# Message layer of a graph network: a PSUM bank per slot, and GpSimd's gathers and scatters in blocks of four

## The chip, the cores and the metric

The kernel runs on 1 core of one Trainium2 chip. The metric is the time of one execution on the device in microseconds; lower is better.

## The reference, cut to what matters

Four graph layers are applied to a table of 50,000 nodes with 128 features each, over 25,000 edges sorted by destination; each adds its result to the table and normalizes the rows. The change is in the last one, the message layer:

```python
x = _layernorm(x + _L3_gnn_ref(x, edge_weight, src, dst, L3_gnn_Wm, ...), axis=-1)

def _L3_gnn_ref(z, edge_weight, edge_src, edge_dst, Wm, bm, W1, b1, W2, b2):
    Wd, Ws, ww = (Wm[:H], Wm[H:2 * H], Wm[2 * H])
    msgs = z[edge_dst] @ Wd + z[edge_src] @ Ws + edge_weight[:, None] * ww[None, :] + bm
    agg = jax.ops.segment_max(msgs, edge_dst, num_segments=n)
    agg = jnp.where(deg[:, None] > 0, agg, jnp.zeros((), dtype=z.dtype))
    hidden = jax.nn.relu(z @ W1a + agg @ W1b + b1)
    return hidden @ W2 + b2
```

## The kernel before, in words

The program runs its stages one after the other: a prelude (weights folded, tables of edges), the dense pass over all nodes together with the first edge layer, then the edge layers PNA, attention and message. Nodes without an edge are finished in the dense pass; an edge layer computes the rows that have edges. `message_edges` is the last stage.

It walks the edges backward in 49 groups of 512 (`GROUP`), each four tiles of 128 edges. For a group: four gathers on GpSimd fetch the source rows (`gsrc.tile`, one indirect DMA of 128 rows of 512 bytes each, line 1603); SyncE loads the group's own rows, the edge weights and a row of flags. TensorE turns the source rows (TURN_SRC) and own rows (TURN_OWN) with four transposes each, ScalarE copies them to SBUF (COPY_SRC, COPY_OWN), TensorE forms the messages (SOURCE, two products of 512 columns in fp32, listed as two instructions each), VectorE takes the running maximum with one scan (SCAN), which starts from the last column of the group before. TensorE multiplies own rows (OWN, with the constant rows) and the maximum (HIDDEN) into one bank, ScalarE applies the ReLU, TensorE makes the output rows (PRODUCT, eight instructions of 128 columns, line 335), VectorE adds the own rows (RESIDUAL), and the layer norm follows: SQUARE (ScalarE), SUM (VectorE), ROOT (ScalarE), NEWTON (four small operations, VectorE), SCALE (four activations, ScalarE). Last, GpSimd writes the rows with four indirect DMAs (SCATTER0 to SCATTER3, line 2491).

All tiles have two copies, called slots; group n uses slot n mod 2. Of the PSUM banks, those for the hidden and the output rows have two copies, the one that takes the turned source rows and then the messages (`bank_src`) and the one for turned own rows (`bank_own`) have one each.

The order on every engine comes from a software pipeline, `pipelined`. `AT` gives each step a planned time after its group's start, `PERIOD` the distance between two groups. A step's place in a round is its time modulo the period, its age in rounds the quotient; every engine issues its own steps in that order, and waits on semaphores settle the rest. The planned times have no effect but this order. So before the change, in round n (the number is the group's age):

```
GpSimd   FETCH0(0) SCATTER0(4) FETCH1(0) SCATTER1(4) FETCH2(0) SCATTER2(4) FETCH3(0) SCATTER3(4)
TensorE  TURN_SRC(1) TURN_OWN(1) PRODUCT(2) SOURCE(1) OWN(1) HIDDEN(1)
ScalarE  SCALE(3) COPY_SRC(1) COPY_OWN(1) SQUARE(2) ROOT(2) RELU(1)
VectorE  RESIDUAL(2) SCAN(1) SUM(2) NEWTON(2)
SyncE    LOAD_OWN(0) LOAD_ROWS(0)
```

FETCH0 waits until the slot's earlier source rows are turned, SCATTER0 until its group is scaled (`norm.normed`), SCALE until the slot's earlier scatters have landed. The steady rounds run in a loop on each engine; the first and the last rounds are written out.

Of the kernel before, what the change touches and what calls it, by code (L numbers as in the profile page):

```python
# [87 lines left out]
def wait(eng, sem, count):  # L88

    if not (isinstance(count, int) and count == 0):  # L90
        eng.wait_ge(sem, count)  # L91
# [73 lines left out]
def backward(ap):  # L165

    return ap[:, ::-1]
# [150 lines left out]
def transpose_tiles(pe, out, rows, ident):  # L318

    for t in range(TPG):  # L320
        mm = pe.transpose(out[:, t:GROUP:TPG], rows[:, t * P:(t + 1) * P], ident[:])  # L321
    return mm
# [2106 lines left out]
def message_edges(nc, A, D, W, Ed, plan):  # L2429


    S, rounds = plan.ES, plan.E_ROUNDS
    mem = Mem(nc)
    rows = lambda n: [mem.sb(f"m_{n}{s}", [P, GROUP]) for s in range(S)]
    src, own, srcT, ownT, mx, h, y, x4 = (rows(n) for n in ("src", "own", "srcT", "ownT", "mx", "h", "y", "x4"))
    wrow = [mem.sb(f"m_wrow{s}", [1, GROUP]) for s in range(S)]
    low = [mem.sb(f"m_low{s}", [P, GROUP], BF16) for s in range(S)]
    bank_src, bank_own = mem.ps("m_bsrc"), mem.ps("m_bown")
    bank_hid, bank_out = ([mem.ps(f"m_b{n}{s}") for s in range(S)] for n in ("hid", "out"))
    norm = Norm(mem, "mn", S, 1, by_scalar=True)  # L2440
    gsrc = Gather(mem, "mg", S, Ed.src_first, D["x3"], src)
    (src_turned, src_copied, made, scanned, own_turned, own_copied, own_made, hidden, relued, out_made, residual, own_loaded,
# [8 lines left out]

    (FETCH0, FETCH1, FETCH2, FETCH3, LOAD_OWN, LOAD_ROWS, TURN_SRC, COPY_SRC, SOURCE, SCAN, TURN_OWN, COPY_OWN, OWN, HIDDEN,
     RELU, PRODUCT, RESIDUAL, SQUARE, SUM, ROOT, NEWTON, SCALE, SCATTER0, SCATTER1, SCATTER2, SCATTER3) = range(26)
    AT = (0, 2.5, 5.1, 7.6, 5.6, 6.1, 11.7, 14.2, 14.9, 17.1, 12.2, 14.7, 16.8, 18.6, 19.8, 22.9, 25, 25.9, 28.5, 29.4, 29.8,
          33.3, 41.9, 44.4, 47, 49.5)
    PERIOD = 10.2
    FETCH = (FETCH0, FETCH1, FETCH2, FETCH3)
    SCATTER = (SCATTER0, SCATTER1, SCATTER2, SCATTER3)

    with nc.Block() as block:  # L2460
        @block.sync
        def _(sp):
            def step(k, s, i):
                g = group(i, s)
                if k == LOAD_OWN:
                    wait(sp, own_turned[s], i)
                    wait(sp, residual[s], i)
                    mem.settle(sp)
                    sp.dma_start(own[s][:], tin[g + plan.DG]).then_inc(own_loaded[s], 16)
                if k == LOAD_ROWS:  # L2470
                    wait(sp, made[s], i)
                    wait(sp, scanned[s], i)
                    mem.settle(sp)
                    sp.dma_start(wrow[s][:], A["w_row"][bass.ds(g, 1), :]).then_inc(row_loaded[s], 16)
                    sp.dma_start(low[s][:], low_row[:, bass.ds(g * GROUP + 1, GROUP)].to_broadcast([P, GROUP])).then_inc(row_loaded[s], 16)

            pipelined(sp, plan.EG, S, PERIOD, AT, step)

        @block.gpsimd
        def _(pool):  # L2480
            def step(k, s, i):
                if k == FETCH0:
                    wait(pool, src_turned[s], i)
                if k in FETCH:
                    gsrc.tile(pool, s, FETCH.index(k), group(i, s))
                if k == SCATTER0:
                    wait(pool, norm.normed[s], i + 1)
                if k in SCATTER:
                    t = SCATTER.index(k)
                    at = group(i, s) * TPG + t  # L2490
                    pool.indirect_dma_start(  # L2491
                        out=D["out"], out_offset=bass.IndirectOffsetOnAxis(ap=Ed.out_first[:, at:at + 1], axis=0),
                        in_=x4[s][:, t * P:(t + 1) * P], in_offset=None, bounds_check=plan.N - 1, oob_is_err=False,
                    ).then_inc(stored[s], 16)

            pipelined(pool, plan.EG, S, PERIOD, AT, step, tail=rounds)
            for s in range(S):
                pool.wait_ge(stored[s], in_slot(plan.EG, S, s) * 16 * TPG)

        @block.tensor  # L2500
        def _(pe):
            def step(k, s, i):
                if k == TURN_SRC:
                    gsrc.arrived(pe, i, s)
                    wait(pe, scanned[s - 1], before(i, s))
                    transpose_tiles(pe, bank_src, src[s], W.ident).then_inc(src_turned[s], 1)
                if k == SOURCE:
                    wait(pe, src_copied[s], i + 1)
                    wait(pe, row_loaded[s], 32 * i + 32)
                    pe.matmul(bank_src[:], W.msg_src[:], srcT[s][:], start=True, stop=False)  # L2510
                    pe.matmul(bank_src[:], W.msg_w[:], wrow[s][:], start=False, stop=True).then_inc(made[s], 1)  # L2511
                if k == TURN_OWN:
                    wait(pe, own_loaded[s], 16 * i + 16)
                    wait(pe, own_copied[s - 1], before(i, s))
                    transpose_tiles(pe, bank_own, own[s], W.ident).then_inc(own_turned[s], 1)
                if k == OWN:
                    wait(pe, own_copied[s], i + 1)
                    wait(pe, relued[s], i)
                    wait(pe, residual[s], i)
                    pe.matmul(bank_hid[s][:], W.w1a_edge[:], ownT[s][:], start=True, stop=False)  # L2520
                    const_rows(pe, bank_out[s], W, C_MSG).then_inc(own_made[s], 1)
                if k == HIDDEN:
                    wait(pe, scanned[s], i + 1)
                    pe.matmul(bank_hid[s][:], W.w1b[:], mx[s][:], start=False, stop=True).then_inc(hidden[s], 1)  # L2524
                if k == PRODUCT:
                    wait(pe, relued[s], i + 1)
                    rows_matmul(pe, bank_out[s], h[s], W.w2_msg[:], stop=True).then_inc(out_made[s], 1)

            pipelined(pe, plan.EG, S, PERIOD, AT, step)

        @block.scalar
        def _(act):
            def step(k, s, i):
                if k == COPY_SRC:
                    wait(act, src_turned[s], i + 1)
                    wait(act, made[s], i)
                    act.copy(srcT[s][:], bank_src[:]).then_inc(src_copied[s], 1)
                if k == COPY_OWN:
                    wait(act, own_turned[s], i + 1)
                    wait(act, own_made[s], i)  # L2540
                    act.copy(ownT[s][:], bank_own[:]).then_inc(own_copied[s], 1)
                if k == RELU:
                    wait(act, hidden[s], i + 1)
                    wait(act, out_made[s], i)
                    act.activation(h[s][:], bank_hid[s][:], ACT.Relu, bias=W.b1_msg[:, 0:1]).then_inc(relued[s], 1)  # L2545
                if k == SQUARE:
                    wait(act, residual[s], i + 1)
                    norm.square(act, i, s, 0, tiles(y[s][:]))
                if k == ROOT:
                    norm.root_by_scalar(act, i, s, 0)  # L2550
                if k == SCALE:
                    wait(act, norm.inverted[s], 4 * i + 4)
                    wait(act, stored[s], i * 16 * TPG)
                    norm.scale_by_scalar(act, i, s, 0, x4[s], y[s])

            pipelined(act, plan.EG, S, PERIOD, AT, step)

        @block.vector
        def _(dve):
            norm.set_eps(dve, began)  # L2560
            dve.memset(mx[S - 1][:], 0.0).then_inc(began, 1)
            dve.wait_ge(began, S + 1)

            def step(k, s, i):
                if k == SCAN:
                    wait(dve, made[s], i + 1)
                    wait(dve, scanned[s - 1], before(i, s))
                    wait(dve, row_loaded[s], 32 * i + 32)
                    wait(dve, hidden[s], i)
                    dve.tensor_tensor_scan(backward(mx[s]), backward(low[s]), backward(bank_src), mx[s - 1][:, 0:1],  # L2570
                                           ALU.add, ALU.max).then_inc(scanned[s], 1)
                if k == RESIDUAL:
                    wait(dve, own_loaded[s], 16 * i + 16)
                    wait(dve, out_made[s], i + 1)
                    wait(dve, norm.normed[s], i)
                    dve.tensor_tensor(y[s][:], bank_out[s][:], own[s][:], ALU.add).then_inc(residual[s], 1)  # L2576
                if k == SUM:
                    norm.sums(dve, i, s, 0)
                if k == NEWTON:
                    norm.wait_for_root(dve, i, s, 0)  # L2580

            pipelined(dve, plan.EG, S, PERIOD, AT, step)
# [96 lines left out]
```

## Time and profile before

| | us |
|---|---|
| median of 3 runs | 3875.34 (3873.74 to 3887.8) |
| span of the profiled execution | 3856.9 |
| message layer in it | 3247 to 3857, 49 groups |
| GpSimd busy in this layer | 389 of 610 |
| TensorE busy in this layer | 435 of 610 |
| VectorE, ScalarE busy in this layer | 158, 181 of 610 |

The time of a run is the device's, and lies some 18 us over the span from the first to the last instruction of the profiled execution. PE is TensorE, PEld its weight loads, DVE VectorE, ACT ScalarE, POOL GpSimd, SP SyncE. In a timeline the first number is the start in us from the start of the span, the second the duration; "x4" are four instructions merged in one row; what stands in brackets is how long the engine sat idle before it and what ended that. The ends of matmuls are modelled. A releaser named as a DMA that had long landed, or as "remote", is one that the profile could not tell.

### The profile page before, as it was taken

To read this page: it belongs to the slowest core of one execution; us is meant where nothing else is said; L and a number is where in the kernel's file an instruction comes from. 1 tells how busy PE (TensorE), PEld (TensorE's weight loads), DVE (VectorE), ACT (ScalarE), POOL (GpSimd) and SP (SyncE) were. 2 spreads that over 40 slices of the span, in tenths; PEclk is the share of its full clock that TensorE was granted. 3 is DMA by queue.
4 is the path that set the end of the run, shared out by engine and by line. 5 is a ranking of instruction groups with operands and counts; after the bars stand their busy time and mean duration, and the time that the engine had idled before them with its cause. 6 is when DMAs were issued, how large, how long until landed. Compare 5 with 4: busy or idle time off the path is not lost. (4 is left out here: it accounts for less than half of the span.)

```text
span 3856.9 us, 54369 instructions
## 1 busy us (share of the span) xinstructions
PE 3033.4 (79%) x11490; PEld 2023.8 (52%) x11490; DVE 2725.5 (71%) x6900; ACT 2299.0 (60%) x5259; POOL 2523.9 (65%) x2721
## 2 busy tenths in 40 slices
PE   3124149999999998899979999979999996777676
PEld 2012035555555555777759999955555553343333
DVE  3005749999999998777769989969999994222222
ACT  2003039999999999777623333439999994232332
POOL 5750069999999998777534444436666763666665
PEclk7557569999999999899989999989999997777777
DMA  5012025555555554444323343322322321222221
GB/s 190 1 36 90 1 76 171 171 168 169 171 164 175 164 176 141 113 123 119 109 86 112 114 112 110 109 81 72 88 83 84 86 82 44 72 73 72 72 68 46
DMA packets 262118, 404.65 MB, mean 105 GB/s; under 512 B 61938, under 2 KB 104135, under 8 KB 262033
## 3 DMA queue, kind: packets, MB, share of 16 engines
q1 hardware_dynamic: 204920, 304.18, 24.6%
q0 software_dynamic: 44032, 73.90, 8.4%
q10 hardware_dynamic: 13081, 25.69, 2.0%
q14 instruction: 62, 0.51, 0.0%
q8 instruction: 23, 0.38, 0.0%
HBM read 213.15 MB, written 194.37 MB: 106 GB/s over the span
## 5 line engine op out<-in xcount | busy, mean ns | idle before, releaser
L256 POOL TENSOR_TENSOR dn_rstd<-dn_var,w_minus_half 128x4 f32<-128x4 f32 x294 | 292.6, 1002 | 16.7 <-DVE dn_var L241 16.5
L1603 POOL DMA_INDIRECT m_src<-table_x,e_src_first x196 | 191.1, 975 | 127.5 <-issue 52.1
L1603 POOL DMA_INDIRECT p_src<-table_x,e_src x196 | 213.1, 1087 | 93.0 <-issue 53.6
L2491 POOL DMA_INDIRECT out_rows<-m_x,e_out_first x196 | 197.6, 1008 | 94.0 <-issue 65.8
L648 POOL DMA_INDIRECT scratch_node_row<-o_own,e_out x196 | 192.0, 979 | 90.7 <-issue 62.4
L1643 POOL DMA_INDIRECT g_own<-in_x,e_dst x196 | 223.9, 1142 | 36.9 <-issue 36.9
L2576 DVE TENSOR_TENSOR m_y<-m_bout,m_own 128x512 f32<-128x512 f32 x49 | 33.9, 692 | 294.3 <-DMA a_typ<-in_type_row 166.3
L1603 POOL DMA_INDIRECT a_src<-table_x,e_src x196 | 200.9, 1025 | 47.6 <-issue 37.5
L1634 POOL DMA_INDIRECT g_src<-scratch_wide,e_src x196 | 192.0, 980 | 58.8 <-issue 46.0
L1409 PE MATMUL n_banks<-w_gru_both,d_xT 128*128 128x256 f32 x784 | 223.6, 430 | 8.6 <-ACT d_xT L1446 8.6
L1409 PEld LDWEIGHTS n_banks<-w_gru_both,d_xT 128*128 128x128 f32 x784 | 192.9, 327 | 71.3 <-ACT d_xT L1446 68.6
L1970 POOL TENSOR_TENSOR pn_rstd<-pn_var,w_minus_half 128x4 f32<-128x4 f32 x49 | 51.1, 1043 | 256.9 <-DVE pn_var L241 256.9
L237 ACT ACTIVATE dn_sq<-n_banks 128x512 f32<-128x512 f32 x294 | 180.2, 614 | 62.2 <-DVE n_banks L1550 46.6
L925 ACT COPY s_xT<-s_bturn 128x512 f32<-128x512 f32 x98 | 52.3, 592 | 269.1 <-remote 222.0
L241 DVE TENSOR_REDUCE dn_var<-dn_sq 128x4 f32<-128x516 f32 x294 | 199.6, 680 | 17.6 <-issue 10.3
L2524 PE MATMUL m_bhid<-m_mx,w_w1b 128*128 128x512 f32 x98 | 80.8, 919 | 116.5 <-DVE m_mx L2570 65.2
L1824 PE MATMUL n_banks<-w_own,d_n 128*128 128x384 f32 x392 | 165.6, 572 | 0.0
L2000 PE MATMUL p_bout<-w_post,p_mx 128*128 128x384 f32 x392 | 165.0, 503 | 0.0
L305 ACT ACTIVATE d_x<-d_y,dl_shift,dl_rstd 128x128 f32<-128x128 f32 x392 | 161.7, 486 | 0.0
L2000 PE MATMUL p_bout<-w_post,p_mn 128*128 128x384 f32 x392 | 158.8, 487 | 0.0
L2000 PE MATMUL p_bout<-w_post,p_mean 128*128 128x384 f32 x392 | 158.5, 486 | 0.0
L2000 PE MATMUL p_bout<-w_post,p_var 128*128 128x384 f32 x392 | 158.5, 486 | 0.0
(486 smaller groups left out, 9952.8 us busy)
## 6 DMA issues: line engine op xcount, KB each, us to landing
table_x<-d_x SPq DMA_DIRECT2D x294, 256.0 KB, 2.0
g_src<-in_x_wide SPq DMA_DIRECT2D x97, 262.0 KB
scratch_wide<-g_src SPq DMA_DIRECT2D x97, 262.0 KB
out_rows<-d_x SPq DMA_DIRECT2D x97, 256.0 KB
s_x<-in_x ACTq DMA_DIRECT2D x31, 768.0 KB
table_x<-d_xT SPq DMA_DIRECT2D x49, 256.0 KB
scratch_post<-d_x SPq DMA_DIRECT2D x49, 256.0 KB, 2.0
p_rc<-scratch_rcount SPq DMA_DIRECT2D x49, 256.0 KB
```

Of the source, the lines that this page charges most:

```text
L237: act.activation(self.sq[s][:, :, 0:P], y, ACT.Square, scale=ROOT).then_inc(self.squared[s], 1)
L241: dve.tensor_reduce(self.var[s][:], self.sq[s][:], AX, ALU.add).then_inc(self.summed[s], 1)
L256: pool.tensor_tensor(self.rstd[s][:], self.var[s][:], minus_half[:], ALU.pow).then_inc(self.rooted[s], 1)
L305: ins = act.activation(out[:, c], y[:, c], ACT.Identity, bias=self.shift[s][:, t:t + 1], scale=self.rstd[s][:, t:t + 1])
L648: pool.indirect_dma_start(out=D["node_row"], out_offset=bass.IndirectOffsetOnAxis(ap=Ed.out[:, t:t + 1], axis=0), in_=self.own[:, t, :], i ...
L1409: mm = pe.matmul(pair[s][:, 2 * t * P:2 * (t + 1) * P], xT[s][:, t:GROUP:TPG], W.gru_both[:], start=True, stop=True, skip_group_check=True)
L1603: pool.indirect_dma_start(out=self.rows[s][:, t * P:(t + 1) * P], out_offset=None, in_=self.table, in_offset=bass.IndirectOffsetOnAxis(ap= ...
L1634: pool.indirect_dma_start(out=self.src[s][:, t, :], out_offset=None, in_=self.D["wide"], in_offset=bass.IndirectOffsetOnAxis(ap=self.Ed.sr ...
L1643: pool.indirect_dma_start(out=self.own[:, at * P:(at + 1) * P], out_offset=None, in_=self.A["x"], in_offset=bass.IndirectOffsetOnAxis(ap=s ...
L1824: mm = pe.matmul(wide(t), x1T[s][:, t:GROUP:TPG], W.own[:], start=False, stop=True, skip_group_check=True)
L2000: mm = pe.matmul(bank_out[:, t * GROUP:t * GROUP + SCALERS * P], cols[s][:, t:GROUP:TPG], W.post[:, stat_block(n, 0):stat_block(n, SCALERS ...
L2491: pool.indirect_dma_start(out=D["out"], out_offset=bass.IndirectOffsetOnAxis(ap=Ed.out_first[:, at:at + 1], axis=0), in_=x4[s][:, t * P:(t ...
```

## The change

`bank_src` and `bank_own` get a copy for each slot, which makes eight banks in use. TURN_SRC then waits for the scan of the slot's earlier group, two groups back, and no longer for the scan of the group before; TURN_OWN waits for the copy two groups back. All planned times are new, and the period is 10.3. The order in round n becomes:

```
GpSimd   FETCH0(0) FETCH1(0) FETCH2(0) FETCH3(0) SCATTER0(2) SCATTER1(2) SCATTER2(2) SCATTER3(2)
TensorE  OWN(1) HIDDEN(1) PRODUCT(1) TURN_OWN(0) TURN_SRC(0) SOURCE(0)
ScalarE  ROOT(2) SCALE(2) RELU(1) SQUARE(1) COPY_SRC(0) COPY_OWN(0)
VectorE  NEWTON(2) SCAN(1) RESIDUAL(1) SUM(1)
SyncE    LOAD_OWN(0) LOAD_ROWS(0)
```

```diff
-    bank_src, bank_own = mem.ps("m_bsrc"), mem.ps("m_bown")
-    bank_hid, bank_out = ([mem.ps(f"m_b{n}{s}") for s in range(S)] for n in ("hid", "out"))
+    bank_src, bank_own, bank_hid, bank_out = ([mem.ps(f"m_b{n}{s}") for s in range(S)] for n in ("src", "own", "hid", "out"))
...
-    AT = (0, 2.5, 5.1, 7.6, 5.6, 6.1, 11.7, 14.2, 14.9, 17.1, 12.2, 14.7, 16.8, 18.6, 19.8, 22.9, 25, 25.9, 28.5, 29.4, 29.8,
-          33.3, 41.9, 44.4, 47, 49.5)
-    PERIOD = 10.2
+    AT = (0, 1.29, 2.58, 3.87, 1.7, 1.9, 8.2, 9.15, 9.9, 12.1, 7.5, 9.8, 12, 13.6, 14.8, 15.6, 17.9, 18.8, 19.6, 20.8,
+          21.1, 22.1, 25.8, 27.1, 28.4, 29.7)
+    PERIOD = 10.3
...
                     gsrc.arrived(pe, i, s)
-                    wait(pe, scanned[s - 1], before(i, s))
-                    transpose_tiles(pe, bank_src, src[s], W.ident).then_inc(src_turned[s], 1)
+                    wait(pe, scanned[s], i)
+                    transpose_tiles(pe, bank_src[s], src[s], W.ident).then_inc(src_turned[s], 1)
...
                     wait(pe, own_loaded[s], 16 * i + 16)
-                    wait(pe, own_copied[s - 1], before(i, s))
-                    transpose_tiles(pe, bank_own, own[s], W.ident).then_inc(own_turned[s], 1)
+                    wait(pe, own_copied[s], i)
+                    transpose_tiles(pe, bank_own[s], own[s], W.ident).then_inc(own_turned[s], 1)
```

The other lines of the diff put `bank_src[s]` and `bank_own[s]` in the place of `bank_src` and `bank_own` in SOURCE, COPY_SRC, COPY_OWN and SCAN. The times in `AT` belong to FETCH0 to FETCH3, LOAD_OWN, LOAD_ROWS, TURN_SRC, COPY_SRC, SOURCE, SCAN, TURN_OWN, COPY_OWN, OWN, HIDDEN, RELU, PRODUCT, RESIDUAL, SQUARE, SUM, ROOT, NEWTON, SCALE and SCATTER0 to SCATTER3, in this order.

## Rows read from the trace of the kernel before

**Rows 1.** Table by stage: TensorE, its weight loads, VectorE, ScalarE, GpSimd busy; clock; DMA.
```profile
2700.00:3200.00 500.00, 460.97 (x1879) 253.18 (x1879) 484.45 (x1084) 478.67 (x883) 340.38 (x340) 1.00 0.29 83
...
3247.00:3857.00 610.00, 434.80 (x1225) 233.70 (x1225) 158.14 (x344) 181.18 (x442) 388.65 (x392) 0.76 0.24 68
```

**Rows 2.** Groups of the message stage: busy time, mean of one, idle time before and its releasers.
```profile
L2491 POOL DMA_INDIRECT out_rows<-m_x,e_out_first x196 | 197.6, 1008 | 94.0 <-issue 65.8 <-ACT m_x L268 28.2
L1603 POOL DMA_INDIRECT m_src<-table_x,e_src_first x196 | 191.1, 975 | 127.5 <-issue 52.1 <-PE m_bsrc L321 51.7 <-POOLq L2610 9.1
```

**Rows 3.** Timeline of GpSimd: start, duration, [idle before <- releaser].
```profile
3638.76 0.97 POOL L1603 DMA_INDIRECT m_src<-table_x,e_src_first  x1 [3.25 <-PE m_bsrc L321]
3640.38 1.01 POOL L2491 DMA_INDIRECT out_rows<-m_x,e_out_first  x1 [0.64 <-issue]
...
3658.56 1.01 POOL L2491 DMA_INDIRECT out_rows<-m_x,e_out_first  x1 [0.31 <-issue]
3661.95 0.97 POOL L1603 DMA_INDIRECT m_src<-table_x,e_src_first  x1 [2.38 <-PE m_bsrc L321]
3664.34 1.01 POOL L2491 DMA_INDIRECT out_rows<-m_x,e_out_first  x1 [1.42 <-ACT m_x L268]
...
3709.97 0.98 POOL L1603 DMA_INDIRECT m_src<-table_x,e_src_first  x1 [2.39 <-PE m_bsrc L321]
```

**Rows 4.** Timeline of a slow round, 3646 to 3662 us.
```profile
3646.44 2.13 PE L335 MATMUL m_bout<-w_w_msg,m_h 128*128 128x128 f32 x8
...
3649.36 1.12 PE L2511 MATMUL m_bsrc<-m_wrow,w_msg_w 1*128 1x512 f32 x2
...
3651.81 0.69 DVE L2576 TENSOR_TENSOR m_y<-m_bout,m_own 128x512 f32<-128x512 f32 x1 [5.66 <-DMA a_typ<-in_type_row]
...
3656.85 1.28 DVE L2570 TENSOR_TENSOR_SCAN m_mx<-m_low,m_mx,m_bsrc 128x512 f32<-128x512 bf16 x1 [4.34 <-remote]
...
3658.19 2.07 PE L2524 MATMUL m_bhid<-m_mx,w_w1b 128*128 128x512 f32 x2 [6.33 <-issue]
...
3661.65 0.69 ACT L2545 ACTIVATE m_h<-m_bhid,w_b_msg 128x512 f32<-128x512 f32 x1 [2.70 <-PE m_bhid L2524]
```

**Rows 5.** Timeline of the end of the layer.
```profile
3820.31 2.23 PE L335 MATMUL m_bout<-w_w_msg,m_h 128*128 128x128 f32 x8 [2.88 <-ACT m_h L2545]
...
3827.46 0.60 PE L321 MATMUL m_bsrc<-w_ident,m_src 128*128 128x128 f32 x4
...
3828.40 2.13 PE L335 MATMUL m_bout<-w_w_msg,m_h 128*128 128x128 f32 x8
...
3830.30 0.98 POOL L2491 DMA_INDIRECT out_rows<-m_x,e_out_first  x1 [3.18 <-ACT m_x L268]
...
3833.82 1.13 PE L2524 MATMUL m_bhid<-m_mx,w_w1b 128*128 128x512 f32 x2
...
3835.72 2.13 PE L335 MATMUL m_bout<-w_w_msg,m_h 128*128 128x128 f32 x8 [0.78 <-ACT m_h L2545]
...
3838.79 0.63 ACT L237 ACTIVATE mn_sq<-m_y 128x512 f32<-128x512 f32 x1 [1.95 <-DVE m_y L2576]
...
3843.28 0.98 POOL L2491 DMA_INDIRECT out_rows<-m_x,e_out_first  x1 [0.80 <-ACT m_x L268]
```

**Rows 6.** Timeline of the prelude, 108 to 122 us.
```profile
109.22 0.80 PE L582 MATMUL u_bank<-f_linT,f_post 128*128 128x128 f32 x2 [58.67 <-issue]
...
110.73 0.98 POOL L648 DMA_INDIRECT scratch_node_row<-o_own,e_out  x1 [0.30 <-issue]
...
114.41 0.29 DVE L531 COPY w_post<-u_bank 128x128 f32<-128x128 f32 x1 [5.24 <-remote]
```

**Rows 7.** Timeline of the beginning of the layer.
```profile
3250.94 0.95 POOL L1603 DMA_INDIRECT m_src<-table_x,e_src_first  x1 [0.30 <-issue]
...
3253.48 1.12 PE L321 MATMUL m_bsrc<-w_ident,m_src 128*128 128x128 f32 x4 [21.70 <-DMA m_src<-table_x,e_src_first]
```

**Rows 8.** Chain of waits: start, duration, engine, tile, line.
```profile
3486.90 2.00 PE m_bsrc L2511 x2
```

More of the change, by code:

```diff
@@ L2509, in step @@
                     wait(pe, row_loaded[s], 32 * i + 32)
-                    pe.matmul(bank_src[:], W.msg_src[:], srcT[s][:], start=True, stop=False)
-                    pe.matmul(bank_src[:], W.msg_w[:], wrow[s][:], start=False, stop=True).then_inc(made[s], 1)
+                    pe.matmul(bank_src[s][:], W.msg_src[:], srcT[s][:], start=True, stop=False)
+                    pe.matmul(bank_src[s][:], W.msg_w[:], wrow[s][:], start=False, stop=True).then_inc(made[s], 1)
                 if k == TURN_OWN:
                     wait(pe, own_loaded[s], 16 * i + 16)
-                    wait(pe, own_copied[s - 1], before(i, s))
-                    transpose_tiles(pe, bank_own, own[s], W.ident).then_inc(own_turned[s], 1)
+                    wait(pe, own_copied[s], i)
+                    transpose_tiles(pe, bank_own[s], own[s], W.ident).then_inc(own_turned[s], 1)
                 if k == OWN:
@@ L2536, in step @@
                     wait(act, made[s], i)
-                    act.copy(srcT[s][:], bank_src[:]).then_inc(src_copied[s], 1)
+                    act.copy(srcT[s][:], bank_src[s][:]).then_inc(src_copied[s], 1)
                 if k == COPY_OWN:
@@ L2540, in step @@
                     wait(act, own_made[s], i)
-                    act.copy(ownT[s][:], bank_own[:]).then_inc(own_copied[s], 1)
+                    act.copy(ownT[s][:], bank_own[s][:]).then_inc(own_copied[s], 1)
                 if k == RELU:
@@ L2569, in step @@
                     wait(dve, hidden[s], i)
-                    dve.tensor_tensor_scan(backward(mx[s]), backward(low[s]), backward(bank_src), mx[s - 1][:, 0:1],
+                    dve.tensor_tensor_scan(backward(mx[s]), backward(low[s]), backward(bank_src[s]), mx[s - 1][:, 0:1],
                                            ALU.add, ALU.max).then_inc(scanned[s], 1)
```

## The prediction

> **What bounds the kernel now.** I read the page first, then the table by stage, the groups of the message stage, and last the timelines of GpSimd and of single rounds. The message layer is the last stage, from 3247 us to the end of the span: 49 groups in 610 us. Its own limits lie lower. GpSimd issues eight indirect DMAs for each group, four gathers and four scatters, and one starts every 1.30 us (0.98 or 1.01 us and 0.30 us of issue) [rows 2, 3], so eight cost 10.4 us. TensorE's round, at the pace of the end of the layer, is 7.3 to 8.1 us (from the start of one PRODUCT to the next, 3820.31, 3828.40, 3835.72) [rows 5]. What is measured is neither. GpSimd's pauses come once in two groups: from 3661.95 to 3709.97 there are two such pairs, 24.0 us each, so 12.0 us for one group [rows 3].
>
> Why 24.0 and not 20.8? One round in two is slow, and it is not slow in TensorE's own rows. PRODUCT at 3646.44 is listed for 2.13 us, to 3648.57, but VectorE's residual, which waits for it, starts at 3651.81, 3.2 us late. The source matmul ends at 3650.48 and the scan starts at 3656.85, 6.4 us late. The hidden matmul ends at 3660.26 and the ReLU starts at 3661.65. Elsewhere they are on time: PRODUCT's end at 3837.85 is followed by the residual (0.69 us) and by the square at 3838.79 [rows 5]. So in one stretch TensorE's results reach the others 3 to 6 us late, and then all at once. I looked for what else has that rhythm and found GpSimd. It issues without a pause from 3640.38 to 3659.57; the lateness is there from about 8 us into that run, and it is gone at 3661.65, 2.1 us after the run ends [rows 3, 4]. At the end of the layer, where no gathers are left and GpSimd pauses for 3 us between groups of four scatters, the rounds are fast [rows 5]. The prelude shows the same with nothing else going on: under an unbroken row of scatters, one product of 0.80 us at 109.22 is copied at 114.41, 4.4 us late [rows 6]. I don't know the mechanism; that GpSimd's unbroken issue delays TensorE's results is what I infer from the three places.
>
> The loop is then: GpSimd runs two rounds, TensorE falls behind, GpSimd has to wait until a source buffer is turned (FETCH0, 2.4 or 3.3 us) and then for a scaled group (1.4 or 0.6 us), the late results arrive, and it starts again [rows 3]. 16 issues, 20.8 us, and the two waits without their ordinary 0.3 us give 24.0.
>
> **The change, part by part.** *The banks.* TURN_SRC no longer waits for the scan of the group before, TURN_OWN no longer for its copy. Neither wait ended last: in both orders TURN_SRC stands behind HIDDEN of the group before, which waits for the same scan, and the copy of own rows is done several steps earlier. Value 0, and if it were not, the scan's 1.28 us would be the most in a round [rows 4]. The waits that stay are two groups old.
>
> *GpSimd's order.* The same eight issues, 10.4 us; at the head of the layer gathers already follow each other at 0.95 + 0.30 us, so bunching neither costs nor saves [rows 7]. SP's loads stand earlier in a round and wait for work two groups old; the plan leaves 5.8 us from LOAD_OWN to TURN_OWN, and a gather of the same rows needs 2.5 [rows 7]. Value 0; with the cover gone, 2.5 us at the worst, once.
>
> *The depth.* Before, group n is scattered four rounds after its fetch (41.9 of 10.2). Now it is two rounds after (25.8 of 10.3), right behind the four gathers of group n+2. FETCH0's wait for the turned source becomes loose, since TURN_SRC now stands in the same round as the fetch. SCATTER0's wait becomes the short leash. The last gather is planned at 3.87 and its rows can be turned 2.5 us after its start (3250.94 to 3253.48) [rows 7], so 19.4 us are left to the scatter at 25.8. The chain at its best needs 14.3: turns 1.0, copy 0.6 (taken as the square, 0.63), source 2.1, scan 1.3, hidden 1.1, ReLU 0.7, PRODUCT 2.1, then 5.4 us from PRODUCT's end (3837.85) to the scatter (3843.28) [rows 4, 5]. Two or three results that are 3 to 6 us late use up the 5 us between. What is queued behind SCATTER0 on GpSimd is the whole of the next group's fetch.
>
> *TensorE's order.* Before, a round was TURN_SRC, TURN_OWN, PRODUCT of the older group, SOURCE, OWN, HIDDEN: the turns covered the ReLU, PRODUCT covered the copy. Now it is OWN, HIDDEN, PRODUCT of one group, TURN_OWN, TURN_SRC, SOURCE of the next. Between HIDDEN and PRODUCT nothing covers the ReLU: 0.78 us. And ScalarE has SQUARE ahead of COPY_SRC; it ends 1.6 us after PRODUCT (3837.85 to 3839.42), the copy takes 0.6 more, so SOURCE starts 2.2 us after PRODUCT's end, while the eight turns need 1.0 (from 3827.46 to the next PRODUCT, 3828.40, they are done) [rows 5]. A fast round becomes 2.2 + 2.1 (source, two parts of up to 1.12) + 1.3 (scan) + 1.1 (hidden) + 0.8 (ReLU) + 2.1 (PRODUCT) = 9.6, with a few hundredths at each hand-over 9.7 us, against a mean of 7.7 of the two rounds shown [rows 4, 5]. That is 2.0 us more, under GpSimd's 10.4, but TensorE has to catch up after each slow stretch, and there it counts.
>
> **The sum.** I take the pair of rounds as the unit, 24.0 us now. Lower bound: only the fast round of a pair gets longer: 26.0. Both do: 28.0. From GpSimd's side: two rounds of issues, 20.8, then it stops at SCATTER0; the late results arrive 2.1 us later, and if PRODUCT is the one that was late, 5.4 us of residual, square, sum, root, Newton and scale follow before it may go on: 28.3. Before, the wait was for a turn, behind which nothing had to be worked off; that is the new wait in place of the old. The bounds are 26.0 and 28.3; I take the middle, 27.1, as the late result will sometimes be through the chain already. That is 3.1 us for a pair. The last three groups run behind the last gather as before, which leaves 23 pairs: 23 x 3.1 = 71 us. Head and tail stay: the first turn waits for the first four gathers, and 5.4 us and four scatters follow the last PRODUCT, in both. The profiled execution's span of 3857 us becomes 3928; the median of the runs lies 18 us over that span (3875.3 against 3856.9), so the forecast is 3946 us, 1.8% slower. Its own range by the bounds is 46 to 99 us more, 3921 to 3974.
>
> On this lateness the trace is set against the Trainium skill. Its page "TensorE: Matmul & The Clock Gate", section "The cost: per-tile semaphore tail", counts some 26 ns for each increment of a semaphore by a matmul; the trace shows 3 to 6 us, so the measurement decides. By the page there would be no slow round, and the sum would be GpSimd's 10.4 us a group, the first rival's time.
>
> **The rivals.**
> *Faster: the late results go away.* If they hang on gathers and scatters taking turns, or on a queue of TensorE work that the new waits keep short, each round costs the larger of 10.4 and 9.7 us: 46 rounds x (12.0 - 10.4) = 74 us less, 3801 us. It decides as soon as a pair is under 24.0 us, so with half of the lateness gone it is already faster. For it: TensorE's work fits. Against it: a row of scatters alone [rows 6] shows the same delay, and so 10.4 us of issue without a stop is not short enough, since the first late result comes some 8 us into a run. A pause that helps must be about 2.1 us; once a round it gives 12.5 us, again no gain.
> *No change.* The added waits fall into the time in which TensorE is held up anyway, and the chain behind SCATTER0 is far enough along: the pair stays at 24.0, 3875 us, within 19.
> *Slower still: the clock.* The granted clock is 0.76 in this stage against 1.00 in the stage before it, where TensorE is busy for 461 of 500 us [rows 1]: it changes between its levels of 1.2 and 2.4 GHz. More waits mean less dense work. Wholly at the lower level, where a product of 512 columns takes 2.0 us, a round is turns 2.0, copy 0.6, source 4.0, OWN and the constants 2.4, hidden 2.1, ReLU 0.8, PRODUCT 2.2 = 14.1 us [rows 4, 5, 8], 46 x 2.1 = 97 us more even with no result late, 3972. The same page of the Trainium skill, section "What's actually happening", says the throttled state is the default and activity lifts it, which speaks against this change; the trace agrees so far that the sparser stage has the lower clock.
>
> **How the numbers follow.** The forecast has a chance of 0.57, the clock 0.08, no change 0.13, faster 0.22. Half a per cent, 19 us, is about what a measurement can tell here. Faster by more than that: 0.22; within: 0.13; slower: 0.65. The range that leaves out no more than 2 in 10 runs from 3815 us, which leaves the full gain of the first rival outside, to 3990 us, which takes in the clock's price and leaves out that price with the lateness on top.
>
> **What would show it.** In the changed kernel's trace of this stage: GpSimd's wait for the turned source (51.7 us in all before [rows 2]) all but gone, and its wait for the scaled rows (28.2 us before) grown to over 100 us; a pause of 4 to 8 us once in two groups, always before a scatter; VectorE's scan and residual still starting 3 us and more behind TensorE's listed ends in the slow rounds; SOURCE starting about 2 us after PRODUCT's end in fast ones. The prediction is wrong if GpSimd's runs go on over three groups and more without a pause, if the late results are gone while it issues back to back, or if the pair stays at 24 us.

## The result, and the profile after

The changed kernel takes 3942.21 us (median of four runs, 3932.49 to 3949.09), the kernel before on the same chip 3876.0 us (3873.74 to 3887.8): a ratio of 1.0166, 95% interval 1.014 to 1.0192, 66 us slower. The forecast was 3946. The profiled execution's span went from 3856.9 to 3936.8 us.

The table by stage, for the message layer of the changed kernel (start:end, length, then busy time of TensorE, its weight loads, VectorE, ScalarE and GpSimd, granted clock, DMA share, GB/s):

```profile
3247.00:3937.00 690.00, 494.58 (x1225) 241.80 (x1225) 163.09 (x343) 184.95 (x442) 383.77 (x392) 0.68 0.21 60
```

Against [rows 1] the work is the same (1225 matmul instructions, 392 indirect DMAs in 384 us). The granted clock fell from 0.76 to 0.68, so that TensorE's same instructions are busy for 495 us and not 435.

The groups of this stage, GpSimd's two kinds of DMA:

```profile
L2490 POOL DMA_INDIRECT out_rows<-m_x,e_out_first x196 | 195.5, 997 | 237.8 <-ACT m_x L268 186.0 <-issue 51.7
L1603 POOL DMA_INDIRECT m_src<-table_x,e_src_first x196 | 188.8, 963 | 68.5 <-issue 59.5 <-POOLq L2609 9.1
```

Against [rows 2] the idle time has changed sides. The gathers' wait for a turned source is gone (51.7 to nothing), and the scatters' wait for scaled rows is 186.0 us and not 28.2.

What ended VectorE's and TensorE's waits (idle us, count, longest):

```profile
PE m_bsrc L2509 <- ACT m_srcT L2536: 74.6, 27, 9.6
...
DVE m_y L2575 <- PE m_bout L335: 197.9, 35, 10.0
```

TensorE now waits 74.6 us, 27 times, for COPY_SRC before SOURCE, the hand-over that nothing covers in the new order. It is 1.18 us in the fast round below; the longest, 9.6, has a late result in it. The second row is VectorE's wait for PRODUCT; VectorE is not what bounds the stage.

A fast round of the changed kernel in the timeline (PRODUCT, residual, square, copy, SOURCE, next PRODUCT):

```profile
3604.94 2.13 PE L335 MATMUL m_bout<-w_w_msg,m_h 128*128 128x128 f32 x8 [0.78 <-ACT m_h L2544]
...
3607.16 0.69 DVE L2575 TENSOR_TENSOR m_y<-m_bout,m_own 128x512 f32<-128x512 f32 x1 [5.50 <-PE m_bout L335]
...
3607.89 0.63 ACT L237 ACTIVATE mn_sq<-m_y 128x512 f32<-128x512 f32 x1 [3.00 <-issue]
...
3608.42 0.57 ACT L2536 COPY m_srcT<-m_bsrc 128x512 f32<-128x512 f32 x1
...
3609.12 1.12 PE L2509 MATMUL m_bsrc<-m_srcT,w_msg_src 128*128 128x512 f32 x2 [1.18 <-ACT m_srcT L2536]
...
3612.54 1.02 POOL L2490 DMA_INDIRECT out_rows<-m_x,e_out_first  x1 [0.98 <-ACT m_x L268]
...
3614.74 2.13 PE L335 MATMUL m_bout<-w_w_msg,m_h 128*128 128x128 f32 x8 [0.78 <-issue]
```

PRODUCT ends at 3607.07 and the residual starts at 3607.16: on time. SOURCE starts 2.05 us after PRODUCT's end, behind the square and the copy, and the next PRODUCT 9.80 us after the first.

The slow round right behind it, in the same timeline:

```profile
3620.29 1.38 PE L2510 MATMUL m_bsrc<-m_wrow,w_msg_w 1*128 1x512 f32 x2
...
3626.08 1.28 DVE L2569 TENSOR_TENSOR_SCAN m_mx<-m_low,m_mx,m_bsrc 128x512 f32<-128x512 bf16 x1 [5.51 <-remote]
...
3627.41 2.08 PE L2523 MATMUL m_bhid<-m_mx,w_w1b 128*128 128x512 f32 x2 [3.21 <-DVE m_mx L2569]
...
3631.89 0.95 POOL L1603 DMA_INDIRECT m_src<-table_x,e_src_first  x1 [0.30 <-issue]
...
3634.30 0.69 ACT L2544 ACTIVATE m_h<-m_bhid,w_b_msg 128x512 f32<-128x512 f32 x1 [12.27 <-DMA a_src<-table_x,e_src]
3635.04 2.24 PE L335 MATMUL m_bout<-w_w_msg,m_h 128*128 128x128 f32 x8 [5.55 <-ACT m_h L2544]
...
3642.77 1.02 POOL L2490 DMA_INDIRECT out_rows<-m_x,e_out_first  x1 [9.93 <-ACT m_x L268]
```

SOURCE's end is listed at 3621.67 and the scan starts 4.4 us later. HIDDEN's end is listed at 3629.49 and the ReLU starts 4.8 us later. GpSimd issues from 3612.54 to 3632.84 without a pause, and the ReLU is released 1.5 us after that run ends. Only then can PRODUCT, residual, norm and scale follow, and GpSimd stands for 9.93 us before SCATTER0. The next rounds, from the same timeline, have nothing late and are slow for another reason:

```profile
3646.86 2.23 PE L335 MATMUL m_bout<-w_w_msg,m_h 128*128 128x128 f32 x8 [0.78 <-ACT m_h L2544]
...
3651.47 2.08 PE L2509 MATMUL m_bsrc<-m_srcT,w_msg_src 128*128 128x512 f32 x2 [0.68 <-ACT m_srcT L2536]
...
3660.87 1.53 PE L335 MATMUL m_bout<-w_w_msg,m_h 128*128 128x128 f32 x5 [0.78 <-ACT m_h L2544]
...
3668.98 1.02 POOL L2490 DMA_INDIRECT out_rows<-m_x,e_out_first  x1 [3.90 <-ACT m_x L268]
```

SOURCE's first part takes 2.08 us where it took 1.12. The table by stage for this one round, from PRODUCT to PRODUCT, has a granted clock of 0.50, the level of 1.2 GHz:

```profile
3646.86:3660.87 14.01, 12.56 (x25) 5.64 (x26) 3.33 (x7) 3.78 (x9) 9.22 (x10) 0.50 0.27 69
```

The round is 14.0 us, the rival's 14.1, and GpSimd stands for 3.90 us before SCATTER0 with nothing late. From SCATTER0 at 3327.89 to the one at 3897.64 there are 42 rounds, 13.57 us each.

Call a group late when its scan, ReLU, residual or one of its two copies starts more than 1 us after the listed end of its matmul, its engine idle for as long. Over these 43 groups (the fifth to the 47th) that is so in only 15; in the kernel before it is in 42 of the same 43. GpSimd stands for over 2 us before SCATTER0 in 29 of them. Fifteen of these stops are those of the late groups, 3.6 to 9.9 us, 97 us in all; the other 14, of 2.3 to 4.2 us, have nothing late in their group and add up to 49 us. Most of the rest of the 186.0 is at the head and tail of the layer. And it matters whether GpSimd stood before: after 1.31 us or less the next group is late in 11 of 13 cases, after more than 2 us in 4 of 30, and in these four it is a copy alone, late in the same stretch as a result of the group before.

### The profile page after: what moved, and what is told of

It is laid out like the page before. It is cut to its first block and busy times, and to the rows that moved or that the text cites. A ratio compares the mean times of both kernels' runs of the same rounds, so it can differ in the third digit from the quotient of the medians.

```text
span 3936.8 us, 54406 instructions
## 1 busy us (share of the span) xinstructions
PE 3094.5 (79%) x11490; PEld 2032.4 (52%) x11490; DVE 2730.2 (69%) x6900; ACT 2307.2 (59%) x5259; POOL 2518.9 (64%) x2721
## 5 line engine op out<-in xcount | busy, mean ns | idle before, releaser
L2490 POOL DMA_INDIRECT out_rows<-m_x,e_out_first x196 | 195.5, 997 | 237.8 <-ACT m_x L268 186.0
L2544 ACT ACTIVATE m_h<-m_bhid,w_b_msg 128x512 f32<-128x512 f32 x49 | 33.7, 688 | 226.8 <-PE m_bhid L2523 164.7
L335 PEld LDWEIGHTS m_bout<-w_w_msg,m_h 128*128 128x128 f32 x392 | 95.1, 327 | 125.9 <-ACT m_h L2544 122.7
L335 PE MATMUL m_bout<-w_w_msg,m_h 128*128 128x128 f32 x392 | 107.9, 442 | 66.1 <-ACT m_h L2544 64.5
```

The costliest lines, as they stand in the source:

```text
L335: mm = pe.matmul(out[:, t * P:(t + 1) * P], cols[:, t:GROUP:TPG], w, start=start, stop=stop, skip_group_check=True)
L2490: pool.indirect_dma_start(out=D["out"], out_offset=bass.IndirectOffsetOnAxis(ap=Ed.out_first[:, at:at + 1], axis=0), in_=x4[s][:, t * P:(t ...
```

## The experiments

Each ratio is to the kernel before, run on the same chip. "Round" is mine: from FETCH0 of the fifth group to FETCH0 of the 45th, over 40, in the one profiled execution. "Clock" is the granted clock from 3300 to 3600 us. "Late" is mine too: how many of TensorE's semaphore increments between 3300 and 3600 us are recorded more than 0.3 us after the listed end of their instruction, and their median delay. The trace does not record every increment (108 of some 149 before, 106 of 132 changed), so "late groups" counts by the waiters instead, as above: late groups of the 43 from the fifth to the 47th. e1, e2, e3 and p1 shared a chip, as did p2 and the three n runs, and o1, q1, q2 and s1. The three n runs leave the message layer's scatters out, so its rows of the output are not written.

| run | what | us | ratio (95%) | round | clock | late | late groups |
|---|---|---|---|---|---|---|---|
| before | | 3876.0 | 1 | 12.1 | 0.75 | 57, 2.9 us | 42 |
| changed | | 3942.21 | 1.0166 (1.014 to 1.0192) | 13.7 | 0.68 | 24, 4.4 us | 15 |
| e1_banks | banks alone | 3857.79 | 0.999 (0.998 to 1.0001) | 12.2 | 0.75 | 56, 4.5 us | 41 |
| e2_blocks | GpSimd's blocks alone | 3909.47 | 1.0127 (1.011 to 1.0144) | 13.2 | 0.77 | 38, 9.5 us | 43 |
| o1_order | order of the other engines, banks | 3922.01 | 1.0117 (1.0093 to 1.014) | 13.3 | 0.71 | 20, 5.2 us | 15 |
| e3_deeper | changed, scatters a round later | 3911.51 | 1.0132 (1.0115 to 1.0149) | 13.1 | 0.72 | 23, 2.3 us | 14 |
| n1_noscatter | before, no scatters | 3644.54 | 0.9429 (0.9413 to 0.9445) | 7.5 | 1.00 | 0 | 0 |
| n2_noscatter_after | changed, no scatters | 3778.77 | 0.9781 (0.9764 to 0.9797) | 10.4 | 0.86 | 0 | 0 |
| n3_compute | before, computing for scatters | 3704.21 | one run | 9.1 | 0.94 | 0 | 0 |
| p1_pause | before, 2.35 us of break | 3872.72 | 1.003 (1.0019 to 1.0042) | 12.5 | 0.77 | 0 | 0 |
| p2_pause_short | before, 1.3 us of break | 3832.23 | 0.992 (0.9904 to 0.9937) | 11.6 | 0.75 | 84, 2.4 us | 38 |
| q1_pause_after | changed, 1.3 us of break | 3889.12 | 1.0038 (1.0027 to 1.005) | 12.8 | 0.68 | 16, 2.1 us | 14 |
| q2_blocks_pause | blocks alone, 1.3 us of break | 3836.76 | 0.9892 (0.9868 to 0.9915) | 11.7 | 0.75 | 75, 2.8 us | 40 |
| s1_spread | before, a memset after each DMA | 3899.13 | 1.0063 (1.0046 to 1.0079) | 12.7 | 0.75 | 34, 7.4 us | 40 |

**e1_banks: the banks alone.** The changed kernel with the old times:

```diff
-    AT = (0, 1.29, 2.58, 3.87, 1.7, 1.9, 8.2, 9.15, ...
-    PERIOD = 10.3
+    AT = (0, 2.5, 5.1, 7.6, 5.6, 6.1, 11.7, 14.2, ...
+    PERIOD = 10.2
```

> The banks alone: the order before the change, with a bank per slot for source and own rows. Theory of the prediction (late results, leash, order): neither of the removed waits ended last, so 3876 us within 19, and the late results stay. Rival (the banks pay or cost): if TensorE's turns could start earlier, a round loses up to 1.3 us, 60 us less, about 3816.

0.999: the banks are worth nothing that a measurement can tell.

**e2_blocks: four gathers, then four scatters, and nothing else.** In the kernel before, the order of GpSimd alone. SCATTER0 stays four rounds after its fetch.

```diff
-    AT = (0, 2.5, 5.1, 7.6, ...
-          33.3, 41.9, 44.4, 47, 49.5)
+    AT = (0, 1.3, 2.6, 3.9, ...
+          33.3, 46, 47.3, 48.6, 49.9)
```

> GpSimd's blocks alone: four gathers, then four scatters, still of the group four rounds older; every other engine as before. Theory of the prediction: issue costs the same and GpSimd still stops only for a turned source, so 3876 us within 19, a pair of rounds 24 us. Rival (bunching itself costs, for instance because the scatters come late for the tiles that wait, or because a row of gathers delays others): a good part of the 66 us, 3900 to 3945.

Bunching was priced at nothing and costs 1.27%, 49 us. In the timeline of e2_blocks:

```profile
3609.14 0.69 DVE L2576 TENSOR_TENSOR m_y<-m_bout,m_own 128x512 f32<-128x512 f32 x1 [11.39 <-DMA a_typ<-in_type_row]
3609.33 0.98 POOL L2491 DMA_INDIRECT out_rows<-m_x,e_out_first  x1 [0.30 <-issue]
3612.79 1.28 DVE L2570 TENSOR_TENSOR_SCAN m_mx<-m_low,m_mx,m_bsrc 128x512 f32<-128x512 bf16 x1 [2.96 <-remote]
...
3615.99 1.06 PE L321 MATMUL m_bsrc<-w_ident,m_src 128*128 128x128 f32 x4
...
3617.32 0.99 POOL L1603 DMA_INDIRECT m_src<-table_x,e_src_first  x1 [7.01 <-PE m_bsrc L321]
```

PRODUCT's last instruction is listed from 3599.82 to 3600.22, and the residual starts at 3609.14, 8.9 us late. The late results are later than before, and GpSimd stands at FETCH0 for 7.01 us where [rows 3] had 2.4 and 3.3. Its whole wait for a turned source is 144.4 us, against 51.7 [rows 2]. The gathers of a block start 1.26 to 1.30 us apart, a hair closer than in [rows 3]; whether that little is what counts, or the two kinds taking turns, no run tells.

**e3_deeper: the changed kernel, scattered a round later.** This lengthens the leash.

```diff
-          21.1, 22.1, 25.8, 27.1, 28.4, 29.7)
+          21.1, 22.1, 36.1, 37.4, 38.7, 40)
```

> The changed kernel with the scatters one round later (group n-3 instead of n-2), nothing else changed. If the short leash at the scatter costs most of the 66 us: GpSimd's wait for scaled rows falls from 186 us to under 60, and the time to 3880 to 3905. If the cost lies in TensorE's order (ReLU and copy uncovered) and in the clock: the wait moves to the turned sources and the time stays at 3925 to 3945.

The wait moved as foreseen: 17.9 us for scaled rows and not 186.0, 132.4 us for the turned source. The time hardly did: 1.0132 against 1.0166, some 13 us, and the two intervals overlap, so the size of this gain is uncertain. Whichever wait GpSimd stands at, it stands for nearly as long.

**o1_order: the order of the other engines.** The changed kernel, but GpSimd takes turns as before, with the scatters three rounds old:

```diff
-    AT = (0, 1.29, 2.58, 3.87, ...
-          21.1, 22.1, 25.8, 27.1, 28.4, 29.7)
+    AT = (0, 2.6, 5.2, 7.8, ...
+          21.1, 22.1, 32.2, 34.8, 37.4, 40)
```

> The changed kernel with GpSimd alternating again (gather, scatter, gather, ...), the scatters of the group three rounds older; banks and the order of the other engines as changed. It is the run with the deeper leash without the blocks. If blocks and order add up (the blocks alone cost 49 us, blocks and order with the same leash 51 us): about the time of the kernel before, 3860 to 3880 beside 3861. If each of them alone costs the whole (the late results pass on whatever holds TensorE up): 3895 to 3915.

1.0117, 45 us by the ratio and 49 by the medians. So the order alone, with scatters three rounds old, costs about what the blocks alone cost (49 us), and the two do not add: 51 us together (e3_deeper), 66 with the short leash. o1 and e3 have the same banks, the same order of the other engines and scatters of the same age, and differ in the blocks alone: 1.0117 and 1.0132, with intervals that overlap. In the new order the blocks cost nothing that these runs can tell. And only 15 groups are late in o1, where 42 were before: what the new order costs is not more lateness.

**n1_noscatter and n2_noscatter_after: both kernels without the message layer's scatters.** This takes GpSimd away as the pace and shows TensorE's own.

```diff
-                if k == SCATTER0:
-                    wait(pool, norm.normed[s], i + 1)
-                if k in SCATTER:
...
-                    pool.indirect_dma_start(
-                        out=D["out"], out_offset=bass.IndirectOffsetOnAxis(ap=Ed.out_first[:, at:at + 1], axis=0),
...
-                    wait(act, stored[s], i * 16 * TPG)
```

> The kernel before without the 196 scatters of the message layer (their rows of the output are not written). GpSimd issues four indirect DMAs a round, 5.2 us. Theory: no unbroken rows of issue, so no late results, and TensorE sets its own pace, 7.7 us a round at the full clock, 49 x (12.0 - 7.7) = 211 us less, about 3665; up to 14 us a round, if the clock is at its lower level. Rival (lateness is TensorE's own): pairs of 24 us with late results stay, about 3870.

> The changed kernel without the 196 scatters. The difference to the same cut of the kernel before is the price of TensorE's and ScalarE's new order by itself: by the sum of the prediction 2.0 us a round, 98 us, about 3763 against 3665. If the order costs nothing, the two are equal.

No result is late in either. The rounds are 7.5 and 10.4 us: the new order costs 134 us (3778.77 less 3644.54), 2.9 us a round, when nothing else sets the pace (2.0 and 98 us were expected). A fast round in the timeline of n2_noscatter_after looks like one of the changed kernel:

```profile
3504.00 2.13 PE L335 MATMUL m_bout<-w_w_msg,m_h 128*128 128x128 f32 x8 [0.78 <-ACT m_h L2535]
...
3508.18 1.12 PE L2500 MATMUL m_bsrc<-m_srcT,w_msg_src 128*128 128x512 f32 x2 [1.18 <-ACT m_srcT L2527]
...
3513.79 2.13 PE L335 MATMUL m_bout<-w_w_msg,m_h 128*128 128x128 f32 x8 [0.78 <-ACT m_h L2535]
```

SOURCE starts at 3508.18, 2.05 us after PRODUCT's listed end, and the next PRODUCT 9.79 us after the first. That is 2.3 us over the 7.5 of n1; the other 0.6 of the 2.9 goes with the clock, 0.86 here and 1.00 in n1.

**n3_compute: GpSimd just as busy, with half of the DMAs.** In the kernel before, each scatter becomes an operation of 128 x 4 elements on GpSimd:

```diff
-                    pool.indirect_dma_start(
-                        out=D["out"], out_offset=bass.IndirectOffsetOnAxis(ap=Ed.out_first[:, at:at + 1], axis=0),
...
+                        wait(pool, padded, (i * S + s) * 4 + SCATTER.index(k) + j)
+                        pool.tensor_tensor(pad[:], W.ones[:, 0:TPG], W.minus_half[:], ALU.pow).then_inc(padded, 1)
```

> The kernel before with a small computing operation of GpSimd (1.0 us) in the place of every scatter (rows of the output not written): GpSimd is as busy as before, but issues only half the indirect DMAs. If it is GpSimd's indirect DMAs that delay TensorE's results: no late results, and GpSimd's 10.4 us a round set the time, some 3800. If any unbroken work of GpSimd does it: slow rounds as before, 3870.

In its timeline GpSimd is as full as before:

```profile
3504.10 1.02 POOL L1603 DMA_INDIRECT m_src<-table_x,e_src_first  x1 [0.19 <-issue]
...
3505.16 1.05 POOL L2490 TENSOR_TENSOR m_pad<-w_ones,w_minus_half 128x4 f32<-128x4 f32 x1
...
3506.06 2.06 PE L335 MATMUL m_bout<-w_w_msg,m_h 128*128 128x128 f32 x8
...
3508.20 0.69 DVE L2571 TENSOR_TENSOR m_y<-m_bout,m_own 128x512 f32<-128x512 f32 x1 [4.89 <-PE m_bout L335]
```

PRODUCT ends at 3508.12 and the residual starts at 3508.20, and so it is throughout: no late result, although GpSimd hardly pauses (busy for 271 of 300 us) and sets the pace with 9.1 us a round. (10.4 and some 3800 us had been expected, too much: a gather and the operation behind it take 2.28 us together.) It is not GpSimd's work that makes TensorE's results late, it is indirect DMAs issued closely. Here they start 2.28 us apart.

**p1_pause and p2_pause_short: a break after each group.** Two such operations in p1, one in p2, behind SCATTER3 in the kernel before:

```diff
+                if k == SCATTER3:
+                    for j in range(2):
+                        wait(pool, padded, (i * S + s) * 2 + 0 + j)
+                        pool.tensor_tensor(pad[:], W.ones[:, 0:TPG], W.minus_half[:], ALU.pow).then_inc(padded, 1)
```

> The kernel before with two small operations on GpSimd (some 1.3 us each with issue) after every fourth scatter, so that its row of indirect DMAs is broken for some 2.6 us once a round; a round of GpSimd is then 13.0 us. Theory (unbroken issue makes TensorE's results late): with a break over 2.1 us the late results are gone, TensorE's rounds are all short, and GpSimd alone sets 13.0 us a round: 3876 + 46 x 1.0 = 3922 us. Rival (the lateness belongs to the clock or to TensorE's own queue): slow rounds with results 3 us and more late are still there, and the time is the larger of the two, anything from 3922 up.

> The kernel before with one such operation after every fourth scatter: a break of 1.6 us between the ends of two issues, a round of GpSimd 11.7 us. If a short break suffices against the lateness: 3876 - 46 x 0.3 = 3862 us, faster than both. If it needs 2.1 us: late results stay and the time is 3876 or up to 60 us more.

The timeline of p1_pause:

```profile
3605.13 1.01 POOL L2492 DMA_INDIRECT out_rows<-m_x,e_out_first  x1 [0.30 <-issue]
3606.14 2.16 POOL L2499 TENSOR_TENSOR m_pad<-w_ones,w_minus_half 128x4 f32<-128x4 f32 x2
...
3608.23 1.95 PE L335 MATMUL m_bout<-w_w_msg,m_h 128*128 128x128 f32 x8
3608.48 1.03 POOL L1603 DMA_INDIRECT m_src<-table_x,e_src_first  x1 [0.18 <-issue]
...
3610.39 0.69 DVE L2581 TENSOR_TENSOR m_y<-m_bout,m_own 128x512 f32<-128x512 f32 x1 [6.73 <-PE m_bout L335]
...
3618.61 2.17 POOL L2499 TENSOR_TENSOR m_pad<-w_ones,w_minus_half 128x4 f32<-128x4 f32 x2
```

Every round is alike, 12.47 us from 3606.14 to 3618.61, and between 3300 and 3600 us no result is late (57 before). The two operations would add 49 x 2.1 = 103 us if GpSimd's issue had been the pace; the kernel is 12 us slower. So before, GpSimd stood for the late results about as long as it now spends on purpose. The DMAs come at nearly the same mean rate in both (eight in 12.5 us, eight in 12.1), so the rate isn't the cause; the run without a break is. The 2.35 us are also just over the time after which late results come: 2.1 us after the end of GpSimd's run in [rows 4], and 2.2 us after it in o1_order (the three increments of the last section).

With one operation the kernel is 0.8% faster than before: 11.6 us a round. Late results have not become fewer: 84 increments are late and not 57, though 38 groups and not 42 are late by over 1 us, and the median fell to 2.4 us. They no longer stop GpSimd for long: it stands for 8.8 us in all for a turned source, 51.7 before.

**q1_pause_after and q2_blocks_pause: the same break elsewhere.** One operation behind SCATTER3, in the changed kernel and in e2_blocks.

> The changed kernel with one small operation of GpSimd after every fourth scatter (a break of 1.3 us, a round of GpSimd 11.4 us). Theory: late results shrink as they did in the kernel before (29 us faster there), so it becomes faster than the changed kernel by 30 to 60 us, 3865 to 3895 beside 3861 of before. If the loss of the change is TensorE's order and the clock alone: no gain, 3920 to 3940.

> GpSimd's blocks in the kernel before's order, with the same break after every fourth scatter. If the blocks cost because they bring the indirect DMAs closer together (1.27 us a piece against 1.30) and so make the late results later: the break takes the cost away, 3830 to 3845, close to the 3832 of the break without blocks. If the blocks cost by when the gathers stand in the round: 49 us over that run, 3880.

The changed kernel goes from 1.0166 to 1.0038; with blocks alone it goes from 1.0127 to 0.9892. In the timeline of q2_blocks_pause results are still late (the ReLU at 3615.44 waited 4.88 us), but FETCH0 stands for only 1.05 us behind the operation:

```profile
3613.66 1.05 POOL L2499 TENSOR_TENSOR m_pad<-w_ones,w_minus_half 128x4 f32<-128x4 f32 x1
3615.44 0.69 ACT L2550 ACTIVATE m_h<-m_bhid,w_b_msg 128x512 f32<-128x512 f32 x1 [4.88 <-DMA a_src<-table_x,e_src]
3615.76 1.02 POOL L1603 DMA_INDIRECT m_src<-table_x,e_src_first  x1 [1.05 <-DMA r_wt<-in_w_row]
...
3625.75 1.05 POOL L2499 TENSOR_TENSOR m_pad<-w_ones,w_minus_half 128x4 f32<-128x4 f32 x1
```

So what the blocks cost, they cost only while GpSimd's issue is unbroken: it is the price of later results and of nothing else in the blocks. The order of the other engines is another matter: with the break in both, the changed kernel is 1.5% slower than q2 (1.0038 less 0.9892, some 57 us; 52 by the medians), and that is the order with its short leash, since the banks are worth nothing. Nor is it more lateness: 14 of 43 groups are late in q1, 40 in q2, and q2 is the faster one.

**s1_spread: the same time, spread.** In the kernel before, a memset of 128 x 1 on GpSimd behind every indirect DMA:

```diff
+                if k in SCATTER:
+                    j = SCATTER.index(k)
+                    wait(pool, padded, (i * S + s) * 4 + j)
+                    pool.memset(pad[:, 0:1], 0.0).then_inc(padded, 1)
```

> The kernel before with a tiny memset (128x1, 0.1 us) on GpSimd after every indirect DMA, so that all are a little further apart, and no longer break. If the spacing is what counts: with 0.1 to 0.15 us for each the round is 11.2 to 11.6 us and the time 3825 to 3840 or lower, as with the one break of 1.3 us. If a break in one piece is needed to let the late results through: 3860 or more.

The timeline of s1_spread shows that the run is no test of spacing:

```profile
3600.30 0.98 POOL L1603 DMA_INDIRECT m_src<-table_x,e_src_first  x1 [0.19 <-issue]
3601.27 0.12 POOL L2504 MEMSET m_pad<- 128x1 f32 x1
...
3601.58 1.01 POOL L2493 DMA_INDIRECT out_rows<-m_x,e_out_first  x1 [0.19 <-issue]
3602.56 0.14 POOL L2500 MEMSET m_pad<- 128x1 f32 x1
3602.89 0.98 POOL L1603 DMA_INDIRECT m_src<-table_x,e_src_first  x1 [0.19 <-issue]
```

The memset takes 0.12 to 0.14 us and fits into the 0.30 us of issue: the DMAs still start 1.28 and 1.31 us apart. That the kernel got 0.6% slower, with a median delay of 7.4 us and not 2.9, I can't explain. Whether a little more room between all DMAs would do what a break does stays open.

**A version that beats both kernels.** q2_blocks_pause (0.9892, interval 0.9868 to 0.9915) and p2_pause_short (0.992, 0.9904 to 0.9937) are both faster than before. Their intervals overlap, so between them there is nothing to choose.

## Why the prediction was right, and where it was not

**The late results: right, and now shown.** The inference from three places of the trace holds. Without the scatters, with half of the DMAs, or with 2.35 us of break, no result is late in 300 us; in every run whose DMAs follow each other with shorter breaks, some are. The figure of 2.1 us for a break that helps was fair: 2.35 us removes the lateness, and the forecast that it gives 12.5 us a round "again no gain" is what p1 measured (12.5, ratio 1.003). What the prediction missed is that half of that break gains, since the lateness need not be gone, only short of the time for which GpSimd stands.

**What the change does to them: missed.** The sum keeps one slow round with late results in every pair. In the changed kernel late groups fell from 42 to 15 of 43. They come almost only where GpSimd had not stopped for over 2 us before SCATTER0, so its own stops seem to act as breaks; that is read from one trace and not tested. Rounds that are slow with nothing late, by the hand-overs of the new order and the lower clock, took the place of the others.

**TensorE's order: right, and priced too low.** Fast round 9.7 us forecast, 9.80 measured; SOURCE 2.2 us behind PRODUCT's end, 2.05 measured; the ReLU's 0.78 us uncovered, as in the rows above. The price was given as 2.0 us a round, and measured with nothing else in the way it is 2.9: 2.3 in the fast round (9.79 against n1's mean of 7.5), and 0.6 as the clock falls with it. It is also the largest part of the loss, 45 to 49 of the 66 us alone (o1_order).

**The banks: right,** nothing (e1_banks).

**"Bunching neither costs nor saves": wrong by itself.** It was priced by the issue times alone, 10.4 us in both orders, and those did stay. But the blocks alone cost 49 us, through the very lateness on which the rest of the argument rested: a residual 8.9 us late in e2_blocks, where [rows 4] had 3.2. The question left out was what the new pattern of issue does to the delay. With the other engines in their new order the step holds all the same: o1 and e3 differ in the blocks alone, and by 6 us, with intervals that overlap.

**The leash: right place, wrong size.** The wait did move to SCATTER0 and grew to 186.0 us, but the stops are of two kinds: 3.6 to 9.9 us with a late result, 2.3 to 4.2 us without. That the leash is short is worth some 13 us of 66 (e3_deeper, with intervals that overlap), and the prediction took the upper bound of the pair, 28.3 us, from it.

**The sum: right, by terms that made up for each other.** The pair was forecast at 27.1 us and two rounds take 2 x 13.57 = 27.1. That agreement is luck in part. The unit was wrong: stops of over 2 us come in 29 of 43 rounds, and those with a late result in 15, about once in three and not once in two. The order's term was too small, the leash's too large, and the clock had no term. The costs are also not additive, as the runs alone and together show (49, 45, 51, 66), so a sum of terms could not have been checked one by one. The 18 us between span and median are no property of the device's time: the changed kernel's profiled run took 3938.54 us with a span of 3936.8, and in every other run on record the time lies 1.7 to 1.9 us over the span. So the profiled execution of the kernel before took some 3859 us, an estimate from its span, and was faster than the four that were timed. The span grew by 80 us and not 71, the median by 66.

**The clock: a rival with 0.08 that is partly true.** The stage's clock fell from 0.76 to 0.68, and rounds of 14.0 us with nothing late exist. The table shows what it belongs to. All runs with the new order of the other engines have 0.68 to 0.72 under GpSimd's full load, and all with the old order 0.75 to 0.77, whether GpSimd issues in blocks or not. So the lower clock goes with the order. How much of its price in the whole kernel is the clock and how much the uncovered hand-overs, I can't separate: no run holds the clock. The page "TensorE: Matmul & The Clock Gate" of the Trainium skill, section "What's actually happening", says that activity lifts the clock, and n1 and n2 agree: 1.00 and 0.86, where TensorE is busy for 293 and 247 us of the same 300.

**What stays open.** What inside the chip delays TensorE's results while indirect DMAs are issued without a break; and whether it is their distance or the break that counts, since n3 changed the number and the distance together and s1 changed neither. Nor does a run separate GpSimd's issue from the transfers that it starts. And why the new order, with as many DMAs, has so few late groups is open.

## What to carry to other kernels

If one engine issues indirect DMAs back to back and others wait for TensorE, compare the waiters' starts with TensorE's listed ends before pricing anything; where they lie microseconds apart, a break of 1.3 us in GpSimd's issue for each group made this kernel 0.8% and 1.1% faster, which no reordering here did. Price a reordering of the issuing engine not only by its issue time but by what the new pattern does to such a delay. And test an order of steps without the engine that paces it: the new order's 2.9 us a round were plain there and more than half hidden behind GpSimd in the whole kernel (o1_order's rounds are 1.2 us longer than before). A delay that one sees in a trace is not yet what a change costs: count how often it occurs in both kernels. Here it had become rarer in the slower one.

## What the runs showed of the hardware that was not expected

TensorE's results can reach other engines 2 to 9.5 us (the medians of the table) after their listed ends while GpSimd issues indirect DMAs 1.3 us apart without a break, and on time when 2.28 us lie between them or 2.35 us after every eight. They then arrive together: in o1_order three of TensorE's increments are recorded at 3630.65, 3630.71 and 3630.77, 2.2 us after a run of GpSimd ends at 3628.49, with delays of 4.76, 3.97 and 3.18 us. A memset of 128 x 1 between two indirect DMAs does not move the start of the next one (1.28 and 1.31 us in s1_spread), as it fits into the 0.30 us of issue. And PRODUCT, eight instructions of 128 columns, takes 2.13 us at a granted clock of 1.00 (3604.94) and 2.23 at 0.50 (3646.86), where products of 512 columns go from 1.12 to 2.08 us.
